# Key and value projections in plain fp32 instead of three fp32r terms

## What is computed

```python
k = (cond @ wk.T + bk).reshape(B, L, H, D).transpose(0, 2, 1, 3)
v = (cond @ wv.T + bv).reshape(B, L, H, D).transpose(0, 2, 1, 3)
scores = jnp.einsum('bhnd,bhld->bhnl', q, k) * inv_sqrt_d + mask[:, None]
attn = jax.nn.softmax(scores, axis=-1)
o = jnp.einsum('bhnl,bhld->bhnd', attn, v)
```

## Time and profile before

| | us |
|---|---|
| median of three runs | 961.38 (958.9 to 964.02) |
| the profiled execution's own time | 964.11 |
| its span, first to last instruction | 962.3 |
| PE, matmuls busy | 876.3 |
| DVE busy | 564.5 |
| ACT busy | 551.5 |

### The profile page before, as it was taken

The page is one execution under the profiler, slowest core; times in us unless marked ns, Lnnn a source line. Parts: engine busy times, 40 slices in busy tenths (PEclk is TensorE's granted clock), DMA queues, the critical chain, the costliest instruction groups (busy, mean ns, idle before and its releaser), DMA issues. The chain is left out here.

```text
span 962.3 us, 19095 instructions
## 1 busy us (share of the span) xinstructions
PE 876.3 (91%) x7675; PEld 760.0 (79%) x7675; DVE 564.5 (59%) x1073; ACT 551.5 (57%) x948; POOL 85.7 (9%) x96
## 2 busy tenths in 40 slices
PE   5944689999999999999999999999999999997875
PEld 3533479898889888988898889898989898976654
DVE  2796455656565656565656565656565656565764
ACT  2512166757576657665666566656665667565322
POOL 1021000000000000000000000000000000016577
PEclk8966799999999999999999999999999999999997
DMA  6009566675757575757575757575757575454042
GB/s 177 12 30 265 148 136 161 133 176 128 177 117 181 126 181 119 177 127 179 118 178 127 179 118 178 128 178 118 179 125 181 117 178 107 97 145 127 20 118 75
DMA packets 70262, 133.32 MB, mean 139 GB/s; under 512 B 24096, under 2 KB 53448, under 8 KB 70088
## 3 DMA queue, kind: packets, MB, share of 16 engines
q1 hardware_dynamic: 66240, 123.61, 54.1%
q0 software_dynamic: 2048, 7.34, 2.8%
q10 hardware_dynamic: 1888, 1.15, 0.4%
HBM read 52.59 MB, written 5.57 MB: 60 GB/s over the span
## 5 line engine op out<-in xcount | busy, mean ns | idle before, releaser
L1267 ACT ACTIVATE probsT<-ps_T 125x448 f32<-125x448 f32 x384 | 195.1, 544 | 176.4 <-PE ps_T L1141 176.3
L1370 DVE CUSTOM_DVE_ANT_0 scores<-ps_scores,mask_sb 112x1500 f32<-112x1500 f32 x128 | 219.7, 1716 | 79.0 <-PE ps_scores L1130 71.1
L1141 PEld LDWEIGHTS ps_T<-ident,scores 112*125 112x125 f32 x1536 | 199.9, 188 | 18.9 <-ACT probsT L1267 4.7
L1141 PE MATMUL ps_T<-ident,scores 112*125 112x112 f32 x1536 | 207.5, 271 | 2.9 <-ACT probsT L1267 2.7
L1257 ACT ACTIVATE scores<-scores,shift 112x1500 f32<-112x1500 f32 x128 | 197.1, 1540 | 1.5 <-DVE shift L1370 1.5
L1118 PE MATMUL ps_proj<-wkvT,room 128*125 128x256 f32 x1152 | 159.7, 289 | 5.9 <-DVE v_sb L1348 5.9
L1110 PE MATMUL ps_proj<-room,wkvT 128*128 128x500 f32 x576 | 157.2, 409 | 5.5 <-DVE room L1353 3.8
L1155 PE MATMUL ps_out<-probsT,v_sb 125*32 125x112 f32 x3072 | 159.6, 260 | 0.0
L1118 PEld LDWEIGHTS ps_proj<-wkvT,room 128*125 128x125 f32 x1152 | 146.8, 189 | 14.7 <-DVE v_sb L1348 6.1
L1155 PEld LDWEIGHTS ps_out<-probsT,v_sb 125*32 125x32 f32 x3072 | 144.2, 110 | 15.5 <-issue 10.7
L1357 DVE SCALAR_TENSOR_TENSOR room<-ps_proj,xbk,room 128x500 fp32r<-128x500 f32 x96 | 70.8, 738 | 125.6 <-ACT room L1252 125.6
(11 more groups left out here) (254 smaller groups left out, 561.7 us busy)
## 6 DMA issues: line engine op xcount, KB each, us to landing
k_stack<-room SPq DMA_DIRECT2D x384, 187.5 KB, 4.0
ctx_rows<-in_ctx SPq DMA_DIRECT2D x48, 500.0 KB
mask_sb<-in_mask_BxSxS_ff SPq DMA_DIRECT2D x32, 328.1 KB
q_stack<-q_hi SPq DMA_DIRECT2D x32, 112.0 KB, 5.4
q_hi<-k_stack SPq DMA_DIRECT2D x4, 448.0 KB, 3.8
q_lo<-k_stack SPq DMA_DIRECT2D x4, 448.0 KB, 4.0
q_stack<-q_lo SPq DMA_DIRECT2D x16, 112.0 KB, 5.4
x_sb<-in_x SPq DMA_DIRECT2D x1, 896.0 KB, 6.9
```

What stands on the lines that cost most here:

```text
L1141: last = nc.tensor.transpose(ps_T[0:LT, (TB * t + k) % 2, j * PN:(j + 1) * PN], scores[:, t % 2, (k * TC + j) * LT:(k * TC + j + 1) * LT], ...
L1267: nc.scalar.activation(probsT[:, t % 2, k * TC:(k + 1) * TC], ps_T[0:LT, (TB * t + k) % 2, 0:TC * PN].rearrange("p (j n) -> p j n", j=TC), ...
L1370: nc.vector.tensor_tensor_reduce(out=split(scores[:, t % 2], NC), in0=ps_scores[0:PN, :, 0:LC], in1=split(mask_sb[:, a], NC), scale=-1.0, ...
```

## The change

The context and the two weights stay whole in fp32. `wkvT` has two slots, `weight_lo` and its semaphore go, and the transposes at L291 and L299 wait for ACT's copy instead. An X unit's result is copied once, by DVE, into `cT`; ACT has no part in it. A K unit is two plain fp32 matmuls, a V unit two times two. The keys are still split into high and low parts behind the K unit, for the scores.

Rooms move in SBUF: `cT` is a tensor of its own, half the size of the two parts before; `room` keeps the keys and gets the one-hot tables; the feed-forward phase puts products and x2T parts over the stack of keys, and gathered rows 0 to 5 into `cT`, 6 and 7 into `wkvT`, 8 to 13 into `v_sb`, 14 and 15 into the stack. With that the waits before the gathers change: the wait for all stacks of keys before gather 3 goes, the one for the values stands before gather 8 (it was 9), and the last wait stands before gather 14 (it was 15) and is for a score of the last batch that comes two later.

```diff
-                        dst = keep["wkvT"][:, 0 if k == XK else 2]
+                        dst = keep["wkvT"][:, 0 if k == XK else 1]
...
-                    if u == 1:
-                        weight_lo(XK)
-                    if u == 2:
-                        weight_lo(XV)
...
                     if j == XG_EARLY:
-                        for p in range(NP):
-                            pool.wait_ge(k_in[p], 16 * STACK * B)
-                    if j == XG_ROOM:
                         pool.wait_ge(values_done, (B - 1) * NP + 2)
-                    if j == NST - 1:
-                        pool.wait_ge(scores_in_psum, (B - 1) * NP + 3)
+                    if j == XG_STACK:
+                        pool.wait_ge(scores_in_psum, (B - 1) * NP + 5)
...
-                        mm = [t for m in range(KT) for t in terms(keep["wkvT"][:, 0, m, e], keep["wkvT"][:, 1, m, e],
-                                                                  cT_hi[:, m, c], cT_lo[:, m, c])]
-                        for i, (w, x) in enumerate(mm):
-                            last = nc.tensor.matmul(ps_proj[:, bank, 0:LC], w, x, start=i == 0, stop=i == len(mm) - 1)
+                        for m in range(KT):
+                            last = nc.tensor.matmul(ps_proj[:, bank, 0:LC], keep["wkvT"][:, 0, m, e], cT[:, m, c], start=m == 0, stop=m == KT - 1)
...
-                            mm = [t for m in range(KT) for t in terms(cT_hi[:, m, c], cT_lo[:, m, c],
-                                                                      keep["wkvT"][:, 2, m], keep["wkvT"][:, 3, m])]
-                            for i, (w, x) in enumerate(mm):
-                                last = nc.tensor.matmul(ps_proj[0:LT, bank, j * D:(j + 1) * D], w, x, start=i == 0, stop=i == len(mm) - 1)
+                            for m in range(KT):
+                                last = nc.tensor.matmul(ps_proj[0:LT, bank, j * D:(j + 1) * D], cT[:, m, c], keep["wkvT"][:, 1, m],
+                                                        start=m == 0, stop=m == KT - 1)
...
-                    if kind == "X":
-                        nc.scalar.activation(cT_hi[:, q, p * LC:(p + 1) * LC], src, ACT.Copy).then_inc(hi_ready, 1)
...
                     if kind == "X":
-                        c = slice(p * LC, (p + 1) * LC)
-                        nc.vector.tensor_tensor(cT_lo[:, q, c], ps_proj[:, bank, 0:LC], cT_hi[:, q, c].bitcast(F32),
-                                                ALU.subtract).then_inc(unit_out, 1)
+                        dve.wait_ge(unit_in_psum, first + at[u] + 1)
+                        nc.vector.tensor_copy(cT[:, q, p * LC:(p + 1) * LC], ps_proj[:, bank, 0:LC]).then_inc(unit_out, 1)
...
-        "wkvT": sb("wkvT", [P, 4, KT, D], F32R),
+        "wkvT": sb("wkvT", [P, 2, KT, D]),
...
-        "room": sb("room", [P, 2 * KT * L + 2 * L], F32R),
+        "cT": sb("cT", [P, KT, L]),
+        "room": sb("room", [P, 2 * L + NST * D], F32R),
```

More of the change, by code:

```diff
@@ L564 @@
 HIDDEN = [("R", k, 0) for k in range(NR)] + [("T", 0, 0), ("T", 1, 0), ("L", 0, 0), ("L", 1, 0), ("C", 0, 0)]
-HI_AT, HI_FIRST = ({u: n for n, u in enumerate(u for u in at if u[0] != "V")} for at in (AT, AT_FIRST))
+HI_AT, HI_FIRST = ({u: n for n, u in enumerate(u for u in at if u[0] == "K")} for at in (AT, AT_FIRST))
 NHI = len(HI_AT)
@@ L588, in projection_room @@
 def projection_room(keep):
-    room, n = keep["room"], KT * L
-    cT_hi, cT_lo = (split(room[:, k * n:(k + 1) * n], KT) for k in range(2))
-    k_hi, k_lo = (room[:, 2 * n + k * L:2 * n + (k + 1) * L] for k in range(2))
+    k_hi, k_lo = (keep["room"][:, k * L:(k + 1) * L] for k in range(2))
     context = split(keep["context"][0:LT], NL)
-    return cT_hi, cT_lo, k_hi, k_lo, context
+    return keep["cT"], k_hi, k_lo, context
 def expert_room(keep):
-    room = {"room": keep["room"][:], "context": keep["context"][:], "w": keep["wkvT"][:].rearrange("p k m d -> p (k m d)"),
-            "v": keep["v_sb"][:, 0].rearrange("p l d -> p (l d)")}
+    room = {"table": keep["room"][:, 2 * L:], "context": keep["context"][:], "w": keep["wkvT"][:].rearrange("p k m d -> p (k m d)"),
+            "cT": keep["cT"][:].rearrange("p m l -> p (m l)"), "v": keep["v_sb"][:, 0].rearrange("p l d -> p (l d)"),
+            "stack": keep["k_stack"][:].rearrange("p k l -> p (k l)")}
     at = dict.fromkeys(room, 0)
@@ L610, in expert_room @@
     return {
[L611 to L614, removed]
+        "pick_r": split(take("table", NST * D), NST),
+        "x2T_hi": split(take("stack", KT * HALF), KT),
+        "x2T_lo": split(take("stack", KT * HALF), KT),
+        "c_stack": take("stack", HALF),
+        "prod": [split(take("stack", BUFS * HALF), BUFS) for k in range(2)],
+        "xg": [take("cT", HALF) for j in range(6)] + [take("w", HALF) for j in range(6, XG_EARLY)]
+        + [take("v", HALF) for j in range(XG_EARLY, XG_STACK)] + [take("stack", HALF, dt=F32) for j in range(XG_STACK, NST)],
         "x2T": split(take("context", 2 * KT * HALF), 2 * KT),
-        "x2T_hi": split(take("w", KT * HALF), KT),
-        "x2T_lo": split(take("w", KT * HALF), KT),
         "c_lo": take("context", T, rows=E, dt=F32R),
@@ L879, in cross_attention_phase @@
         v_sb = keep["v_sb"]
-        cT_hi, cT_lo, k_hi, k_lo, context = projection_room(keep)
+        cT, k_hi, k_lo, context = projection_room(keep)
         k_stack = keep["k_stack"]
@@ L1235, in unit_hi @@
                     kind, p, q = u
-                    if kind in "VRL":
+                    if kind in "XVRL":
                         return
@@ L1241, in unit_hi @@
                     src = ps_proj[:, at[u] % 2, 0:LC]
-                    if kind == "X":
-                        nc.scalar.activation(cT_hi[:, q, p * LC:(p + 1) * LC], src, ACT.Copy).then_inc(hi_ready, 1)
-                    else:
-                        if q == 0:
-                            for k in range(GP):
-                                done = n * 16 * STACK if p == 0 else (n + 1) * 16 * STACK
-                                other = (1 - p) * GP + k
-                                if p == 1 or not isinstance(n, int) or n > 0:
-                                    act.wait_ge(k_in[other], done)
-                        nc.scalar.activation(k_hi[:, q * LC:(q + 1) * LC], src, ACT.Identity,
-                                             bias=keep["xbk"][:, p:p + 1]).then_inc(hi_ready, 1)
+                    if q == 0:
+                        for k in range(GP):
+                            done = n * 16 * STACK if p == 0 else (n + 1) * 16 * STACK
+                            other = (1 - p) * GP + k
+                            if done > 0:
+                                act.wait_ge(k_in[other], done)
+                    nc.scalar.activation(k_hi[:, q * LC:(q + 1) * LC], src, ACT.Identity,
+                                         bias=keep["xbk"][:, p:p + 1]).then_inc(hi_ready, 1)
                 def exponentials(b, t):
@@ L1601, in feed_forward_phase @@
         prod = sb("prod", [P, BUFS, HALF])
-        stacks = keep["k_stack"][:].rearrange("p k l -> p (k l)")
-        prod_hi, prod_lo = (split(stacks[:, k * BUFS * HALF:(k + 1) * BUFS * HALF], BUFS) for k in range(2))
+        prod_hi, prod_lo = e["prod"]
         ffT = sb("ffT", [P, KT, T])
```

18 lines of the change are left out of this document (4 added, 14 removed).

## The result

The changed kernel takes **1004.11 us** (median of 4 runs, 1002.65 to 1005.46), the kernel before, run beside it on the same chip, 960.73 (958.9 to 964.02). The ratio is **1.0435, interval 1.0405 to 1.0465**: slower by 43.4 us, where 43.6 were forecast. The change was run once more in another job, in which the kernel before takes 985.05 us: 1029.39, ratio 1.0441, interval 1.0392 to 1.0491.

The account below looks back on a forecast made before the run. PE was taken as the bound. Batches 43.2, pair waits -3.8, result-unit waits +2.8 and start +1.4 summed to +43.6 us, giving 1005 us on the median, 4.5% slower; range 992 to 1017.

Parts of the forecast that it names:

- The price of plain fp32: Projection matmuls on PE: 0.420 us per instruction at 500 columns, 0.216 at 256, two instructions per matmul.
- The head behind the value product: Extra 0.10 us for units behind the value product, left out for plain fp32; if it stays, +6.4 us.
- The X wait: Value unit between the last two X units: PE's wait goes once ACT is out, -0.16 us a batch.
- R(0): Result unit in seven even batches, waiting for the value unit two before it: +0.4 us each, +2.8.
- The pair ahead of the later R units: Key and value unit before R, 14 times: 3.41 us for 3.17 with its wait, so -3.8 in the sum.
- The 14 batches: Even-paced batches of the loop: 2.88 us more PE work each, less and plus waits at result units.
- The start: First batch's units among weight preparation: +1.4 us for one key and two slow value units, earlier effects hidden.
- Costed at nothing: Weight subtractions, ACT's copies, DVE's copy for its subtraction, moved SBUF places and gather waits: no effect on time.
- Rival 1: Projection groups on PE keep their surplus beyond columns: +0.42 key, +0.43 value unit, about 1040 us; chance 0.05.
- Rival 2: The way out of PSUM through ACT and DVE paces the batches: faster, 954 us; chance 0.02.
- Rival 3: Weight loads pace PE and fall from 1728 to 1152: 63 us less, 899 us; chance 0.01.
- Rival 4: New projection matmuls run as one pass like fp32r: nearly 1 us less per unit, about 780 us; chance 0.01.

Follow-up runs that it names:

- experiment 2: Kernel before, X units copied once by DVE without ACT, low context part left out, fp32r matmuls same in number: 955.75 us, ratio 0.9942.
- experiment 6: Changed kernel with one fp32r matmul in place of each plain fp32 one, low parts left out: 985.41 us, ratio 1.0034, in a job with stalls.
- experiment 1: Changed kernel with POOL's wait for all stacks of keys before gather 3 put back: 1011.25 us, ratio 1.0521 to the kernel before.

## Why the prediction was right, step by step

- **The price of plain fp32** was the step that carried it: 0.420 us at 500 columns and 0.216 at 256, read off L277 and L309. Measured 0.419 and 0.216 (the medians from one instruction to the next inside a unit). The counts, the groups behind transposes (+0.32 and +0.30) and value behind key (+0.30) hold to 0.02 us.
- **The head behind the value product** was left out of the sum and kept as its upper bound. It is there for plain fp32 too: 1.78 and 1.83 us, 0.10 each in two key units and one value unit of every batch. The value unit between X units of the odd batches takes 1.82 us, 0.09 too much as well, though an X unit lies between it and the product. That is about 0.10 x (3 x 14 + 7) = 4.9 us in the 14 batches. The argument for zero, that plain fp32 has no head behind transposes, was right about transposes and said nothing of 32-column tiles.
- **The X wait** went as said: -0.17 in even batches, -0.07 in odd ones, and in even ones another -0.24 at the X units before it, which the sum didn't have (-1.7 in all).
- **R(0)** waits 0.35 us, forecast +0.4. The pair ahead of the later R units has no wait left, as forecast; it takes 3.50 us for 3.41 (the head).
- **The 14 batches**: forecast 14 x 2.88 - 3.8 + 2.8 = 39.3, measured 41.0 to 41.7. The head less the extra X waits would be +3.2; the remaining -0.8 to -1.5 is not taken apart. The text's 3.0 for even batches was met (51.76 for 48.73), its 2.6 for odd ones not: 2.92.
- **The start** came out in size, +1.3 us for +1.4, and not in its parts. The timeline of PE after the change:

```profile
126.27 1.94 PE L1088 MATMUL ps_proj<-cT,wkvT 128*128 128x500 f32 x4
128.05 3.70 PE L1094 MATMUL ps_proj<-wkvT,cT 128*125 128x256 f32 x16
131.58 1.02 PE L1118 MATMUL ps_T<-ident,scores 112*125 112x112 f32 x8
```

  The key unit and the two value units take 5.31 us, where the earlier trace rows had 5.84 and the forecast 7.24. The two value units are the reason, 3.53 us for 4.12: before, they ran mostly at the lower clock in that one execution, and the repeat of the kernel before has them in 3.24 (127.09 to 130.33). The surcharge took a clock state of one trace for a property of the place. What was called hidden ahead of them is not: the key unit starts at 126.27 us for 124.48, and for 125.63 in the repeat. Two errors cancel here.
- **"Costed at nothing"** named the gathers and looked at the right wait, but asked only whether the phase hangs on the gathers' data by way of PE's result chain. It hangs on the block's end, where PE waited 2.93 us for POOL. The phase starts 0.6 to 0.8 us sooner behind the last batch's start, and in the traced pair the clock behind it gave 3.3 more.
- The errors, by the two pairs of traces, are -0.1 at the start, +1.7 to +2.5 in the 15 batches, -1.0 to -3.8 behind them, and cancel in part. Each lies within the bounds that were set but the last, which had no bound, so the closeness of 43.4 to 43.6 is partly luck; an error of 3 us would have been its fair size.
- **The rivals.** Rival 1, that every group keeps its surplus, priced a key unit at +0.42; it came out at +0.31 to +0.33. Rival 2 fell with experiment 2. Rival 3, weight loads, fell with the result: they went down by 34.5 us of busy time while the kernel lost 43, so one of the two measures that the Trainium skill names for TensorE (page "Perfetto Trace Analysis", Identifying the Most-Contended Engine), the busy share of weight loads, points the wrong way in this kernel: 79% before, 72% after. The rival's "more than twice" was misread besides: at L277's 0.377 us for 448 columns, 112 take 0.094, and 0.109 is a sixth more. Rival 4's mechanism fell with the counts, and its price, 780 us, was wrong as well: experiment 6 made the matmuls that cheap and reached no such time.

## What to carry to other kernels

Price an instruction from a place in the same trace where it already runs in the same company, and look at both neighbours: a unit next to the value product had its own price here. Where PE is full, as here, plain fp32 against three fp32r terms was decided by the time from one instruction to the next, and fewer instructions and fewer loads said nothing. Before costing an edit at nothing, ask what each block or barrier behind it waits for last (here a gather's landing), and before counting on less work for the engine that bounds, find what binds next: here 144 us less of PE's work gave 30.

## What was not expected of the hardware

- A group of matmuls on full tiles behind the value product's 32-column tiles takes 0.10 us longer, in fp32r (1.53 for 1.43) and plain fp32 (1.83 for 1.73) alike. It does so ahead of the product too (key unit of the changed kernel, 377.15 to 378.94: 1.79 for 1.69). That the tile shape is the reason is inferred from these places; no run isolates it.
- In two of the jobs every kernel took some 23 us more, with stalls of about 1 us before single matmuls while the gathers ran and no releaser in the trace; the other jobs had none, the last of them on the chip of a job that had. So nothing here shows them to belong to a chip. Ratios of the change agree on both (1.0435 and 1.0441), times don't. What the stalls are stays open.
- The block's end waits for the last gather's data: where PE waited for it, its first matmul behind the block came 1.0 us after the landing, which was 3.2 to 5.1 us after the issue (experiment 1).
- The granted clock at the next phase's start followed the length of PE's idle time ahead of it, as told under experiment 1.
